# ScalarE takes over the two layer norms of the feed-forward part, and three more down projections are split into high and low parts

## The reference

```python
x = _layernorm(x + attention(x, w_qkv))      # x: 8 batches, 512 rows, 128 columns, float32; 16 heads of 8
x = _layernorm(x + ffn(x))

# ffn, for every row s:
scores = sigmoid(x @ gate_w.T)               # 16 experts
_, inds = top_k(scores + expert_bias, 8)
combine = 2.826 * selected / selected.sum()  # zero for the experts that were not chosen
h = silu(x @ w_gate[e].T) * (x @ w_up[e].T)  # for all 16 experts, 128 hidden columns each
y = sum_e combine[e] * (h @ w_down[e].T)  +  shared expert without a weight

def _layernorm(x):                           # no gain, no bias
    return (x - mean(x)) / sqrt(var(x) + 1e-5)
```

## Time and profile before

| | before |
|---|---|
| median of 3 runs | 693.63 us (693.2 to 693.85) |
| the profiled execution | 694.58 us, of which the span of the trace is 692.9 us |
| PE busy | 673.3 us (97%) |
| DVE busy | 577.7 us (83%) |
| ACT busy | 449.8 us (65%) |
| POOL busy | 359.8 us (52%) |

### The profile page before, as it was taken

The page is one execution under the profiler, slowest core; times in us unless marked ns, Lnnn a source line. Parts: engine busy times, 40 slices in busy tenths (PEclk is TensorE's granted clock), DMA queues, the critical chain, the costliest instruction groups (busy, mean ns, idle before and its releaser), DMA issues.

```text
span 692.9 us, 13789 instructions
## 1 busy us (share of the span) xinstructions
PE 673.3 (97%) x3632; PEld 375.1 (54%) x3632; DVE 577.7 (83%) x1109; ACT 449.8 (65%) x860; POOL 359.8 (52%) x405
## 2 busy tenths in 40 slices
PE   7899999999999999999999999999999999999995
PEld 3332343343434443334335777777777777777773
DVE  6979999999999999999954777978788797978664
ACT  2277888888889888888897545445454545445431
POOL 3042434516335253253335767766766767766673
PEclk8579999999999999999999999999999999999998
DMA  5344252422324232241305141150606032150601
GB/s 163 107 154 139 87 162 56 153 69 90 126 85 128 64 121 95 84 156 37 113 3 203 43 176 70 38 223 0 259 0 241 18 141 118 32 227 0 260 0 31
DMA packets 33368, 73.98 MB, mean 107 GB/s; under 512 B 3616, under 2 KB 13088, under 8 KB 29120
## 3 DMA queue, kind: packets, MB, share of 16 engines
q1 hardware_dynamic: 32528, 71.46, 29.3%
q0 software_dynamic: 816, 2.23, 1.2%
HBM read 57.69 MB, written 15.47 MB: 106 GB/s over the span
## 4 chain that ended last, share of the span: by engine, by line
PE 89%; DVE 4%; ACT 3%; POOL 2%; issue 1%; POOLq 0%; DVEq 0%; ACTq 0%
PE ps_sum L1021 18%; PE ps_k L1008 14%; PE ps_bank L1419 10%; PE ps_k L1453 9%; PE ps_k L1419 7%; PE ps_bank L1001 6%; PE ps_bank L1416 5%; PE ps_k L1416 4%; DVE maxima L921 3%; PE ps_k L1449 2%; PE ps_k L1446 2%; PE ps_k L1447 2%; ACT probs L875 2%; PE ps_turned L1001 2%; PE ps_turned L1049 1%
## 5 line engine op out<-in xcount | busy, mean ns | idle before, releaser
L875 ACT ACTIVATE probs<-ps_k 128x512 f32<-128x512 f32 x500 | 264.1, 602 | 47.8 <-PE ps_k L1008 44.1
L921 DVE TENSOR_REDUCE maxima<-ps_bank 128x1 f32<-128x512 f32 x384 | 245.5, 681 | 20.2 <-PE ps_bank L1001 13.4
L1261 POOL TENSOR_TENSOR hidden<-gated,weights 128x512 f32<-128x512 f32 x128 | 188.4, 1488 | 92.7 <-DVE gated L1370 82.1
L1008 PE MATMUL ps_k<-q_aug,k_aug 32*128 32x512 f32 x500 | 150.9, 489 | 1.0 <-ACT probs L875 0.3
L1001 PE MATMUL ps_bank<-k_aug,q_aug 32*128 32x512 f32 x384 | 145.2, 504 | 5.4 <-DVE maxima L921 4.4
L1021 PE MATMUL ps_sum<-probs,v_ones 128*32 128x512 f32 x1024 | 138.5, 613 | 0.3 <-ACT probs L875 0.3
L1008 PEld LDWEIGHTS ps_k<-q_aug,k_aug 32*128 32x128 f32 x500 | 62.1, 185 | 128.6 <-ACT probs L875 116.2
L732 POOL TENSOR_TENSOR shift<-shift_raw,ones 16x128 fp32r<-16x128 f32 x31 | 13.8, 444 | 187.3 <-ACT shift_raw L840 187.3
L1306 ACT ACTIVATE silu<-ps_k 128x512 f32<-128x512 f32 x64 | 38.3, 598 | 80.8 <-PE ps_k L1419 80.6
L921 DVE TENSOR_REDUCE maxima<-ps_turned 128x1 f32<-128x512 f32 x128 | 86.7, 678 | 2.4 <-PE ps_bank L1001 2.1
L1370 DVE TENSOR_TENSOR gated<-silu,ps_bank 128x512 f32<-128x512 f32 x80 | 53.6, 683 | 30.3 <-PE ps_bank L1419 16.5
(11 more groups left out here) (150 smaller groups left out, 940.4 us busy)
## 6 DMA issues: line engine op xcount, KB each, us to landing
weights<-combine_rows SPq DMA_DIRECT2D x32, 1024.0 KB, 7.6
k_aug<-k_rows SPq DMA_DIRECT2D x31, 256.0 KB, 2.7
q_aug<-q_rows SPq DMA_DIRECT2D x31, 256.0 KB, 3.0
q_rows<-qk_high SPq DMA_DIRECT2D x16, 256.0 KB, 3.0
k_rows<-qk_high SPq DMA_DIRECT2D x16, 256.0 KB, 3.2
net_raw<-w_nets POOLq DMA_DIRECT2D x17, 128.0 KB, 2.6
xT_sb<-xT SPq DMA_DIRECT2D x8, 256.0 KB, 2.9
q_rows<-qk_low SPq DMA_DIRECT2D x8, 256.0 KB, 3.0
```

The costliest lines, as they stand in the source:

```text
L875: act.activation(probs[:, t, h, :], score_slot(i, last)[:], ACT.Exp, scale=ATT_SCALE).then_inc(exp_done, 1)
L921: dve.tensor_reduce(maxima[:, parity, TILES * h + t:TILES * h + t + 1], bank("q", (i - UNIT * AHEAD) % SCORES)[:], AX_X, ALU.max).then_inc ...
L1008: return pe.matmul(score_slot(i, last)[:], k_aug[rows, g, t * P:(t + 1) * P], q_aug[rows, g, :], start=True, stop=True).then_inc(scores_k, 1)
L1261: pool.tensor_tensor(hidden[:, s % RING, :], gated[:, s % UP_RING, :], r.weights[:, e, :], ALU.mult).then_inc(hidden_done, 1)
```

## The change

ScalarE now writes both layer norms of the feed-forward part as an activation with a scale and an offset for each row, x * scale + (-mean * scale) (`normalise_by_act`). `x1` for the next batch is written at ScalarE's step 4 (before: VectorE's step 2), `result` at step 10 (before: VectorE's step 13). For that GpSimd's `take_scale` has two more small instructions, `minus_mean` and `offset`. The first batch's x1, made inside the attention part, stays on VectorE.

Nets 2, 12 and 14 are split as well, so 11 of 17 down projections are split. `split_downs` makes the parts of 11 nets in four runs of two instructions (before: of 8 nets in one run of two). The three parts of the selection of experts move from steps 7, 9, 11 to 8, 10, 12. `unit_part` shares the memory of `qk_raw`.

The diff, cut to its core:

```diff
 NETS = EXPERTS + 1
-SPLITS = EXPERTS // 2
+SPLIT_NETS = [1, 2, 3, 5, 7, 9, 11, 12, 13, 14, 15]
+SPLITS = len(SPLIT_NETS)
+SPLIT_RUNS = [(1, 0, 2), (3, 2, 4), (11, 6, 3), (14, 9, 2)]
...
     last.then_inc(r.moments_ready[i], 1)
-def take_scale(pool, r, b, i):
+def take_scale(pool, r, b, i, with_offset=True):
     pool.wait_ge(r.moments_ready[i], b + 1)
+    if with_offset:
+        pool.tensor_tensor(r.minus_mean[:, i, :], r.moments[:, i, :, 0], r.minus_one[:], ALU.mult
+                           ).then_inc(r.minus_mean_ready[i], 1)
...
                        ).then_inc(r.scale_ready[i], 1)
+    if with_offset:
+        pool.wait_ge(r.minus_mean_ready[i], b + i)
+        pool.wait_ge(r.scale_ready[i], b + 1)
+        pool.tensor_tensor(r.offset[:, i, :], r.minus_mean[:, i, :], r.scale[:, i, :], ALU.mult
+                           ).then_inc(r.offset_ready[i], 1)
+def normalise_by_act(act, r, dst, tile, b, i, done):
+    act.wait_ge(r.offset_ready[i], b + i)
+    for t in range(TILES):
+        last = act.activation(dst[:, t, :], tile(t), ACT.Identity, bias=r.offset[:, i, t:t + 1],
+                              scale=r.scale[:, i, t:t + 1])
+    last.then_inc(done, 1)
...
     return lambda t: stream[:, bass.ds(b * TILES + t, 1), :].rearrange("p o d -> p (o d)")
-def normalise_stream(dve, r, stream, b, first):
-    if not first:
-        dve.wait_ge(r.x1_turned, b)
-        dve.wait_ge(r.x1_kept, b)
-    normalise(dve, r, r.x1, stream_tile(stream, b), b, 0, r.x1_ready)
+def normalise_stream(act, r, stream, b):
+    act.wait_ge(r.x1_turned, b)
+    act.wait_ge(r.x1_kept, b)
+    normalise_by_act(act, r, r.x1, stream_tile(stream, b), b, 0, r.x1_ready)
...
             def split_downs():
-                odd = nets_down[:, 1:, :].rearrange("p (j two) d -> p j two d", two=2)[:, :, 0, :]
-                ones = r.ones[:, 0:P].unsqueeze(1).to_broadcast([P, SPLITS, P])
                 pool.wait_ge(r.downs_loaded, DMA)
-                pool.tensor_tensor(downs_high[:], odd, ones, ALU.mult).then_inc(r.downs_high_made, 1)
-                pool.wait_ge(r.downs_high_made, 1)
-                pool.tensor_tensor(downs_low[:], odd, downs_high[:].bitcast(F32), ALU.subtract
-                                   ).then_inc(r.downs_split, 1)
+                for n, j, count in SPLIT_RUNS:
+                    whole = nets_down[:, n:n + 2 * count:2, :] if count == 4 else nets_down[:, n:n + count, :]
+                    ones = r.ones[:, 0:P].unsqueeze(1).to_broadcast([P, count, P])
+                    high, low = downs_high[:, j:j + count, :], downs_low[:, j:j + count, :]
+                    pool.tensor_tensor(high, whole, ones, ALU.mult).then_inc(r.downs_high_made, 1)
+                    pool.wait_ge(r.downs_high_made, SPLIT_RUNS.index((n, j, count)) + 1)
+                    pool.tensor_tensor(low, whole, high.bitcast(F32), ALU.subtract).then_inc(r.downs_split, 1)
...
         stored = sem("stored")
-        LN_IN, TURN_X1, COPY_X1T, GATE, ROUTE, TURN_COMBINE, COPY_COMBINE = 1, 5, 5, 6, 7, 14, 14
-        COPY_Y, TURN_Y, SUM_Y, LN_OUT = 3, 5, 6, 13
+        LN_IN, NORMALISE_IN, TURN_X1, COPY_X1T, GATE, ROUTE, TURN_COMBINE, COPY_COMBINE = 1, 4, 5, 5, 6, 8, 14, 14
+        COPY_Y, TURN_Y, SUM_Y, LN_OUT = 3, 5, 6, 10
...
                 act.copy(yT[:], ps_y[:]).then_inc(y_copied, 1)
+            def finish(b):
+                normalise_by_act(act, r, result, lambda t: y_sum[:, t, :], b, 1, result_ready)
             def round_hidden(b, n, first):
-                j = n // 2
+                j = SPLIT_NETS.index(n)
...
                 if j >= SPLIT_RING:
-                    act.wait_ge(down_done, NETS * b + n - 2 * SPLIT_RING + 1)
+                    act.wait_ge(down_done, NETS * b + SPLIT_NETS[j - SPLIT_RING] + 1)
                 elif not first:
-                    act.wait_ge(down_done, NETS * (b - 1) + n + 2 * (SPLITS - SPLIT_RING) + 1)
+                    act.wait_ge(down_done, NETS * (b - 1) + SPLIT_NETS[j - SPLIT_RING] + 1)
...
                         round_hidden(b, s - 2, first)
+                    if s == NORMALISE_IN and not last:
+                        normalise_stream(act, r, stream, b + 1)
+                    if s == LN_OUT and not first:
+                        finish(b - 1)
...
             copy_y(BATCHES - 1)
+            act.wait_ge(stored, DMA * (BATCHES - 1))
+            finish(BATCHES - 1)
...
                 take_moments(dve, r, lambda t: y_sum[:, t, :], 1)
-            def finish(b):
-                normalise(dve, r, result, lambda t: y_sum[:, t, :], b, 1, result_ready)
             def split_hidden(b, n):
-                j = n // 2
+                j = SPLIT_NETS.index(n)
...
                         take_moments(dve, r, stream_tile(stream, b + 1), 0)
-                    if s == LN_IN + 1 and not last:
-                        normalise_stream(dve, r, stream, b + 1, False)
...
                         sum_y(b - 1)
-                    if s == LN_OUT and not first:
-                        finish(b - 1)
...
             sum_y(BATCHES - 1)
-            dve.wait_ge(stored, DMA * (BATCHES - 1))
-            finish(BATCHES - 1)
...
                         pe.wait_ge(y_copied, b)
-                elif n % 2 == 1:
-                    j = n // 2
+                elif n in SPLIT_NETS:
+                    j = SPLIT_NETS.index(n)
...
             pe.wait_ge(r.downs_loaded, DMA)
-            pe.wait_ge(r.downs_split, 1)
+            pe.wait_ge(r.downs_split, len(SPLIT_RUNS))
```

More of the change, by code:

```diff
@@ L239, in __init__ @@
         self.scale = sb("scale", [P, 2, TILES])
+        self.minus_mean = sb("minus_mean", [P, 2, TILES])
+        self.offset = sb("offset", [P, 2, TILES])
+        self.minus_one = sb("minus_one", [P, TILES])
         self.table = sb("table", [P, 1])
@@ L266, in __init__ @@
         self.scale_ready = [sem("scale_in"), sem("scale_out")]
+        self.minus_mean_ready = [sem("minus_mean_in"), sem("minus_mean_out")]
+        self.offset_ready = [sem("offset_in"), sem("offset_out")]
         self.x1_ready = sem("x1_ready")
@@ L549, in attention @@
         unit_high = sb("unit_high", [P, 2, SEQ], F32R)
-        unit_part = sb("unit_part", [P, 2, SEQ])
         row_kind = sb("row_kind", [P, ROWS // HEAD])
@@ L554, in attention @@
         qk_raw = sb("qk_raw", [P, 2, SEQ])
+        unit_part = qk_raw
         qk_high = sb("qk_high", [P, 2, SEQ], F32R)
@@ L782, in body @@
                     if last and g == 2:
-                        take_scale(pool, r, 0, 0)
+                        take_scale(pool, r, 0, 0, False)
                         keep_x1(pool, r, stream, 0)
@@ L817, in gpsimd @@
             pool.memset(r.minus_half[:], -0.5).then_inc(r.consts_set, 1)
+            pool.memset(r.minus_one[:], -1.0).then_inc(r.consts_set, 1)
             pool.memset(r.epsilon[:], EPS).then_inc(r.consts_set, 1)
             pool.wait_ge(v_pads_set, 1 + GROUPS)
-            pool.wait_ge(r.consts_set, 3)
+            pool.wait_ge(r.consts_set, 4)
             pool.wait_ge(v_staged, 1)
@@ L965, in body @@
                             take_moments(dve, r, stream_tile(stream, 0), 0)
-                            normalise_stream(dve, r, stream, 0, True)
+                            normalise(dve, r, r.x1, stream_tile(stream, 0), 0, 0, r.x1_ready)
                         if at == CONTEXT_AFTER[0] + 2 and not first:
@@ L1186, in splits @@
     def splits(s):
-        n = s - 2
-        return n > 0 and n % 2 == 1
+        return s - 2 in SPLIT_NETS
     with ExitStack() as ctx:
```

## The result

The changed kernel takes **705.87 us** (median of 4, 702.55 to 708.27), the kernel before in the same session 693.74 (693.2 to 694.67). The ratio is 1.017, with a 95% interval of 1.0149 to 1.019: slower. The forecast was 703.4, within 693.5 to 708. The profiled execution took 705.84 us, with a span of 703.9.

What follows compares the result with a forecast made beforehand. TensorE's own list was taken to bound the feed-forward part. Terms -3.7 + 2.8 + 9.1 + 0.5 + 0.3 + 0.8 = +9.8 us gave 704.4 for the profiled execution, 703.4 us as the median, range 693.5 to 708.

Steps and rivals of the forecast that it cites:

- What bounds the kernel: In the feed-forward part TensorE is busy all 39.00 us of a batch; only shortening its list gains, late inputs cost in full.
- The splits: Down projections of nets 2, 12 and 14: each split saves TensorE 0.17 us, 22 of them 3.7 us.
- The start: Start of the feed-forward part: TensorE waits for GpSimd's `downs_split`, 7.6 us instead of 4.8, so +2.8 us.
- rival (c): As (b), and the first wait is not `downs_split` but something that ends by itself: 690.7 us, faster; chance 0.08.
- The clock: TensorE idle 3.3 us at the part's start may drop to half speed, costing 1.7 us or nothing; taken as +0.8.
- The end of each batch: Net 14's `hidden_low` lets GpSimd's `hidden` take the port before `x1T_low`; TensorE waits 1.3 us at 7 places, +9.1 us.
- a late VectorE: At each batch's end VectorE may reach `gated` of net 16 late, adding +0.7 us at most to TensorE's wait.
- The moved norms: On ScalarE: four activations of 0.28 us, 1.1 us, hidden for `x1` with 0.6 to spare; +0.5 us at the very end.
- Rival (d): `x1` also comes late for TensorE's transposes, by some 0.5 us in 7 batches, on top of (a): 706.9 us; chance 0.13.
- Rival (b): At batch ends `x1T_low` follows net 14's `hidden_low` without a `hidden` between; the 7 waits vanish: 694.3 us; chance 0.17.
- The sum: Whole kernel: all terms give +9.8 us, 704.4 for the profiled execution, 703.4 us as the median.
- (a): The forecast itself for the whole kernel, 703.4 us, with its bounds 699.5 to 708; chance 0.62.

Runs made afterwards that it cites:

- e8: Changed kernel with only the 8 odd nets split, so the moved norms and selection alone: 695.03 us, ratio 1.0019 to the kernel before.
- e1: Changed kernel without the split of net 14: 697.98 us, ratio 1.006 to the kernel before.
- e6: Changed kernel without net 14's split, TensorE's wait for `downs_split` moved to net 1's down projection, last `result` normalised on VectorE without `offset`: 691.89 us, ratio 0.996.
- e4: Changed kernel with TensorE waiting for `downs_split` ahead of net 1's down projection, not ahead of the whole part: 699.35 us, ratio 1.0092 to the kernel before.
- e7: Changed kernel with 14 additional, unread matmuls on TensorE ahead of its wait for `downs_split`: 702.23 us, ratio 1.0131 to the kernel before.
- e3: Changed kernel with net 14's `hidden_low` behind `x1T_low` on VectorE and its `hidden_high` behind `x1T_high` on ScalarE: 698.29 us, ratio 1.0071 to the kernel before.
- e2: Changed kernel with `hidden_low` of net 14 behind `x1T_low` on VectorE, ScalarE's order kept: 701.86 us, ratio 1.0116 to the kernel before.
- e9: Changed kernel's splits alone: layer norms stay on VectorE and the selection at steps 7, 9, 11, as in the kernel before: 710.42 us, ratio 1.0234 to it.

## Why the prediction came out right, step by step

- **What bounds the kernel** held: in every version the feed-forward time follows TensorE's own list, its idle pieces and its clock, and a relieved VectorE is worth nothing by itself (e8).
- **The splits** held in size: 0.147 us each in the loop, forecast 0.17. In e1 and e6 two of them save 0.29 per batch.
- **The start** held to the tenth: 7.7 us of splits on GpSimd, forecast 7.6. In e4 the idle time went with the wait for `downs_split`, which rules out rival (c)'s reading of it, and the whole 3.4 us between the two starts came back.
- **The clock** was mis-sized, +0.8 against 2.4. I took half the possible cost, and the length of the earlier fall, 3.4 us; it lasted 6.8, with TensorE busy through most of it. e7 gives 2.45 for it by itself.
- **The end of each batch** held in mechanism and roughly in size, 8.3 of the 9.1 us: `hidden` stands between `hidden_low` and `x1T_low`, and e1 and e3 take 1.03 and 0.92 us a batch away with it. The chain took 2.98 us of the 3.2 worked out, and of the +0.7 for a late VectorE nothing came, since it waits 0.80 us for the product: 1.18 a place where 1.3 was taken. What I left out is ScalarE. I argued as if `hidden_low` on VectorE were all that puts `x1T_low` behind `hidden`; e2 shows that the new `hidden_high` on ScalarE is enough for it.
- **The moved norms** were hidden as worked out, though the activation of 128 columns took 0.48 us (spacing 0.39) where the straight line through 64 and 512 columns gave 0.28. Those two rows have no per-row scale and offset. At the end this is +0.54 of the +1.05; `minus_mean` and `offset` are the rest, as forecast. (The Trainium skill, "ScalarE: Activation LUTs", section "What ACT_TABLE_LOAD costs", gives 186 ns + 93 for each pointer operand + 0.833 per column, which makes, as an estimate, 0.48 us for two such operands and 128 columns; the trace agrees with its 0.48.) What VectorE gains by the moved norms and selection beside the splits (e9) stands in the forecast only as its bound for a late VectorE, for the sum is that of the whole change.
- **Rival (d)** did not come: x1 is waited for only in the first batch of the kernels that start early (e4), 0.7 us. Rival (b) did not come in the changed kernel; e3 makes its condition, VectorE keeping the port, and its waits are gone.
- **The sum** is 2.5 us short of 705.87. The profiled executions differ by 705.84 - 694.58 = 11.26 us, 1.5 more than the forecast's 9.8, most of it the clock. The other 0.95 is what I took off since the profiled execution of before lay above its median; that of the changed kernel lies on its own. The bounds of (a) are not the sum of its terms' bounds, which would be 700.1 to 709.6 instead of 699.5 to 708, and the listed chances make 0.81 for slower, not 0.79; neither touches the result.

## What to carry to other kernels

Ahead of the wait on which the bounding engine starts a batch, put the producers of its input first in every engine's list, and only then work that is due later; a spare of 0.33 us holds no further instruction. Off-loading an engine that is not the bound gains only if its freed time is used: here the move of the norms and the selection was worth nothing alone, and about 4.6 us with the splits beside it. Before making a set-up step longer, move its wait down to where the result is first read; the idle time also costs the clock.

## What the runs showed of the hardware that I had not expected

- In an idle piece of 3.3 us TensorE fell to its lower clock, 1.2 GHz, and kept it for 6.8 us, 5.3 of them with work; that cost 2.4 us. With work in the gap the clock stayed at 2.4 GHz (e7). One of the seven idle pieces of up to 1.6 us in e9 was followed by such a fall too, of 3.4 us; the pieces of about 1 us in the changed kernel were not.
- The same `x1T_low` takes 0.69 us with the port (e3), 1.78 and 1.80 where `hidden` had it first; in e2 `hidden` is listed 0.05 us ahead of it.
- An activation with a scale and an offset for each row takes 0.48 us for 128 columns, one without them 0.61 for 512.
